# The gates of an mLSTM on a Trainium2 core: two batches of a step on two halves of the array's columns, and sizes and logarithms of the first half's gates a step sooner

## The reference, cut to what matters

```
ifg   = concatenate([q, k, v], axis=-1)           # 256 tokens x 768
ig    = (ifg @ igate_w.T + igate_b).T             # 8 heads x 256 tokens
fg    = (ifg @ fgate_w.T + fgate_b).T
log_f = log_sigmoid(fg)
cs    = cumsum(log_f, axis=1)
...                                                # maxima over cs and ig, exp, weighted sums
```

## Time and profile before

| | us |
|---|---|
| median of 3 runs | 1217.89 (1217.12 to 1219.18) |
| the profiled execution | 1213.67 |
| its span in the trace | 1212.1 |
| gates' stage, by the trace | 0 to 68.7 |
| busy in it: TensorE | 44.74 |
| VectorE | 47.01 |
| ScalarE | 18.86 |
| GpSimd | 11.81 |
| mean granted clock in it | 0.90 |
| the same after 68.7, up to 330 | 0.97 |

### The profile page before, as it was taken

One profiled execution on the slowest core, in us unless ns is written; L12 is line 12 of the kernel. 1 busy time (PEld: TensorE's weight loads), 2 busy tenths in 40 slices (PEclk: granted clock), 3 DMA queues, 4 the chain that ended last, 5 costly groups with the idle time before them and its releaser, 6 DMA issues. The chain is left out here.

```text
span 1212.1 us, 28045 instructions
## 1 busy us (share of the span) xinstructions
PE 1108.7 (91%) x9182; PEld 938.6 (77%) x9183; DVE 872.1 (72%) x1983; ACT 700.0 (58%) x1585; POOL 429.7 (35%) x567
## 2 busy tenths in 40 slices
PE   5869998999998899999999889789999999998987
PEld 1346665888887677777766478779999999997986
DVE  5758998766676788888887377457766666664665
ACT  1378996456572667666665543246655555553443
POOL 1237895531202011011130025664533333224654
PEclk8889999999998999999998988879999999998999
DMA  9246651000005446455453047657465555545664
GB/s 322 78 171 238 231 187 54 2 0 0 0 0 115 110 107 124 92 98 115 89 99 55 3 143 266 244 182 252 165 202 172 167 166 171 169 144 165 211 197 135
DMA packets 97678, 164.80 MB, mean 136 GB/s; under 512 B 12044, under 2 KB 72204, under 8 KB 95148
## 3 DMA queue, kind: packets, MB, share of 16 engines
q1 hardware_dynamic: 87756, 136.34, 38.3%
q0 software_dynamic: 9104, 26.49, 6.8%
q10 hardware_dynamic: 720, 0.71, 0.2%
HBM read 103.76 MB, written 33.69 MB: 113 GB/s over the span
## 5 line engine op out<-in xcount | busy, mean ns | idle before, releaser
L1822 DVE TENSOR_REDUCE c_mx<-d_bank 128x2 f32<-128x512 f32 x256 | 164.3, 685 | 18.4 <-PE d_bank L1974 18.0
L1737 ACT ACTIVATE c_probs<-c_t 128x512 f32<-128x512 f32 x248 | 134.7, 598 | 26.9 <-PE c_t L2000 26.1
L2923 ACT ACTIVATE d_g_full<-d_bank,d_e_bias 128x256 f32<-128x256 f32 x156 | 77.5, 497 | 98.6 <-PE d_bank L34 98.6
L32 PE MATMUL d_bank<-de_zt_hi,d_e_hi 128*128 128x256 f32 x312 | 91.1, 292 | 2.0 <-DVE de_zt_lo L2833 2.0
L34 PE MATMUL d_bank<-d_w_hi,d_g_lo 128*128 x312 | 88.2, 283 | 0.0
L33 PE MATMUL d_bank<-d_w_lo,d_g_hi 128*128 x312 | 88.2, 283 | 0.0
L32 PE MATMUL d_bank<-d_w_hi,d_g_hi 128*128 x312 | 88.1, 283 | 0.0
L33 PE MATMUL d_bank<-de_zt_lo,d_e_hi 128*128 128x256 f32 x312 | 87.8, 282 | 0.0
L34 PE MATMUL d_bank<-de_zt_hi,d_e_lo 128*128 128x256 f32 x312 | 87.3, 280 | 0.0
L1670 POOL CAST c_ct_hi<-c_c_raw 128x512 fp32r<-128x512 f32 x15 | 9.2, 611 | 210.0 <-PE c_misc L34 210.0
L3083 POOL DMA_INDIRECT d_w_lo<-d_y_rows,d_pos x64 | 64.3, 1005 | 53.1 <-ACT d_g_hi L3096 23.0
(11 more groups left out here) (424 smaller groups left out, 3763.4 us busy)
## 6 DMA issues: line engine op xcount, KB each, us to landing
d_e_raw<-in_w SPq DMA_DIRECT2D x39, 514.0 KB, 3.8
a_mb<-a_maxima SPq DMA_DIRECT2D x16, 1024.0 KB, 7.5
d_w_hi<-d_zt_kept SPq DMA_DIRECT2D x26, 512.0 KB
d_y_rows<-de_ys SPq DMA_DIRECT2D x39, 256.0 KB, 2.1
d_z_in<-d_z_rows POOLq DMA_DIRECT2D x37, 256.0 KB, 3.7
c_kt<-c_k_hi SPq DMA_DIRECT2D x64, 128.0 KB, 3.1
c_qt<-c_q_hi SPq DMA_DIRECT2D x64, 128.0 KB, 3.8
d_zt_kept<-d_w_hi SPq DMA_DIRECT2D x20, 256.0 KB
```

What stands on the lines that cost most here:

```text
L32: tensor.matmul(out, lhs_hi, rhs_hi, start=start, stop=False)
L1737: act.activation(probs[h % PR][:], t_bank(n, p, k), ACT.Exp).then_inc(exp_done, 1)
L1822: dve.tensor_reduce(mx[n % 2][:, :, k, p:p + 1], s_ps[h % SB], AX.X, ALU.max).then_inc(max_done, 1)
L2923: act.activation(g_full[:, m, :], hid[m][:, 0:TOK], ACT.Gelu, bias=bias[u][:, m:m + 1]).then_inc(gelu_full, 1)
```

## The change

`ROWS` is gone; `HALF` is 64. A step's two batches no longer lie side by side in the 512 columns of 40 partitions, but one on partitions 0 to 39 and the other on 64 to 103 of the same bank, 256 columns wide. Weights are padded to 64 columns. Every matmul of a part becomes two of 256 tokens, first batch and second batch in turn. ScalarE's gates are 128x256 instead of 40x512; `g_rows` and `last_rows` have 128 partitions and half the columns; the bias is loaded twice (two more small DMAs on ScalarE's queue, `gb_loaded` now 64). The placing DMAs are as many and as large, from other partitions. Apart from that, `sizes(0)` goes from i = 6 to i = 5, right behind `scale_by_tanh`, and `logarithms(0)` from behind `gates(5)` to ahead of it.

```diff
-    ROWS = LO + H
+    HALF = P // 2
...
-                queue.dma_start(dst[row:row + H, :], source[at:at + H, b * S:(b + 1) * S]).then_inc(placed, 16)
+                at_b = Mlstm.HALF * b + at
+                queue.dma_start(dst[row:row + H, :], source[at_b:at_b + H, :]).then_inc(placed, 16)
...
-        g_rows = sb("g_rows", [ROWS, (B - rows.LAST) * S])
+        g_rows = sb("g_rows", [P, (STEPS - 1) * S])
...
-            act.dma_start(gb[0:H, :], gate_cols[H:2 * H, :]).then_inc(gb_loaded, 16)
-            act.dma_start(gb[LO:ROWS, :], gate_cols[0:H, :]).then_inc(gb_loaded, 16)
+            for b in range(2):
+                for at, g in ((0, H), (LO, 0)):
+                    act.dma_start(gb[HALF * b + at:HALF * b + at + H, :], gate_cols[g:g + H, :]).then_inc(gb_loaded, 16)
...
-                act.activation(gate_rows(n), g_ps[n % 2][0:ROWS, :], ACT.Identity, bias=gb[:]).then_inc(rows_done, 1)
+                act.activation(gate_rows(n), g_ps[n % 2][:], ACT.Identity, bias=gb[:]).then_inc(rows_done, 1)
...
             for n in range(STEPS):
                 turn(n)
+                if n == 5:
+                    rows.logarithms(act, 0)
                 gates(n)
...
-                if n == 5:
-                    rows.logarithms(act, 0)
...
                 if i == 5:
                     scales(1)
                     scale_by_tanh()
-                if i == 6:
                     rows.sizes(dve, 0)
...
                 for c in range(2):
-                    pe.matmul(g_ps[n % 2][0:ROWS, :], wg[:, 2 + c, :], kt[n % KR][:, c, :], start=(c == 0), stop=False)
+                    for b in range(2):
+                        pe.matmul(g_ps[n % 2][HALF * b:HALF * (b + 1), :], wg[:, 2 + c, :], kt[n % KR][:, c, b * S:(b + 1) * S],
+                                  start=(c == 0), stop=False)
...
                 for c in range(2):
-                    mm = pe.matmul(g_ps[n % 2][0:ROWS, :], wg[:, c, :], qt_all[:, c, n * TOK:(n + 1) * TOK], start=False, stop=(c == 1))
+                    for b in range(2):
+                        mm = pe.matmul(g_ps[n % 2][HALF * b:HALF * (b + 1), :], wg[:, c, :], qt_all[:, c, (2 * n + b) * S:(2 * n + b + 1) * S],
+                                       start=False, stop=(c == 1))
```

More of the change, by code:

```diff
@@ L208, in __init__ @@
         self.cs, self.a, self.m, self.thr = sb("cs", [P, S]), sb("a", [P, S]), sb("m", [P, S]), sb("thr", [P, S])
-        self.last_rows = sb("last_rows", [Mlstm.ROWS, self.LAST * S])
+        self.last_rows = sb("last_rows", [P, S])
         self.placed = [sem(f"placed{k}") for k in range(3)]
@@ L304, in mlstm_gates @@
 def mlstm_gates(nc, src, x_all, tanh_g, ident, half_neg, ctx_t, gate_w, gate_b, qt_all, rows, lora, first):
-    B, S, D, H, J, LO, ROWS = Mlstm.B, Mlstm.S, Mlstm.D, Mlstm.H, Mlstm.J, Mlstm.LO, Mlstm.ROWS
+    B, S, D, H, J, LO, HALF = Mlstm.B, Mlstm.S, Mlstm.D, Mlstm.H, Mlstm.J, Mlstm.LO, Mlstm.HALF
     T = 2 * J
@@ L322, in mlstm_gates @@
         gate_raw = sb("gate_raw", [P, 4])
-        wg_raw, wg = sb("wg_raw", [P, 6, 2 * H]), sb("wg", [P, 4, ROWS])
-        gb = sb("gb", [ROWS, 1])
+        wg_raw, wg = sb("wg_raw", [P, 6, 2 * H]), sb("wg", [P, 4, HALF])
+        gb = sb("gb", [P, 1])
         kt = [sb(f"kt{u}", [P, 2, TOK]) for u in range(KR)]
@@ L335, in mlstm_gates @@
         tz = [[bank(f"tz{u}_{c}", [P, TOK]) for c in range(2)] for u in range(2)]
-        g_ps = [bank(f"g{u}", [P, TOK]) for u in range(2)]
+        g_ps = [bank(f"g{u}", [P, S]) for u in range(2)]
         tok_ps = bank("tok", [P, 2, J, rows.N])
@@ L355, in gate_rows @@
         def gate_rows(n):
-            return g_rows[:, n * TOK:(n + 1) * TOK] if n < PLACED else rows.last_rows[:]
+            return g_rows[:, n * S:(n + 1) * S] if n < PLACED else rows.last_rows[:]
         def place_rows(queue, n):
@@ L450, in _ @@
             act.wait_ge(up_loaded, 16)
-            act.wait_ge(gb_loaded, 32)
+            act.wait_ge(gb_loaded, 64)
             for n in range(STEPS):
                 turn(n)
+                if n == 5:
+                    rows.logarithms(act, 0)
                 gates(n)
```

## The result

| | median, us | runs |
|---|---|---|
| before | 1215.76 | 20 |
| changed | 1212.53 | 20 |

The changed kernel is 3.2 us faster by the medians. The ratio over all runs, which is not the ratio of the medians, is 0.9968, with a 95% interval of 0.9956 to 0.9979: that is 3.9 us, between 2.6 and 5.3. The forecast of 1214.1 has the right sign and the range holds the time, but it rests on a median of before of 1217.89, and twenty runs put that median at 1215.76. The profiled execution of the changed kernel took 1204.82, span 1203.2; it is the fastest of its twenty, by 3.3 us, so its rows show a good execution and not the middle one.

What follows compares the result with a forecast made beforehand. The gates' stage was bounded by the broadcast of the first maxima, later than VectorE's work. Cheaper parts, less the wait before sizes, plus earlier logarithms put the broadcast and first decay 3.8 us earlier: 1217.89 - 3.8 = 1214.1, range 1212.0 to 1217.9.

Steps and rivals of the forecast that it cites:

- The anchor: Whole-kernel time level: median before taken as 1217.89 us, 4.2 above the profiled time, from which the gain was subtracted.
- A part's price: TensorE's context or query part in the gates' stage: 0.96 us at full clock, 1.82 at half, saving 0.79 and 1.6.
- The first two gains: VectorE's two early waits for the turned maxima in the gates' stage: 1.65 us and another 2.57 earlier, 4.2 in all.
- The stall: VectorE's new wait for step 3's placing DMAs before the sizes: 2.3 us, up to 3.2 if half clock lasts.
- The idle time and the clock behind it: TensorE before turn 5: idle 4.7 us from 44.1 to 48.85, then half clock for 4 to 5 us.
- The later chain: SyncE's broadcast of the first maxima, leading to ScalarE's first decay: issued at 60.45 against 64.24, 3.8 us earlier.
- The logarithms ahead: ScalarE's logarithms before the gates of step 5: VectorE's scans start at 53.6 instead of 57.92, its 1.91 us wait gone.
- (a) and (b): VectorE's savings from cheaper parts in the gates' stage: 1.65 us at the first maxima, another 2.57 at the next.
- Carried 1 to 1: From the heads' start to the program's end: the first decay's gain of 3.8 us passes whole into the time.
- Half clock to the end: TensorE's clock stays low until the heads: gain 0 to 1 us; 23 in 100, with gains partly swallowed there.
- Full clock throughout: TensorE's clock never falls in the gates' stage: wait before sizes 1.1 us, total -6.2, 1211.7 us; 6 in 100.
- Rival 1: TensorE's column halves run one after the other, a part costing 1.75 us: +2.7, 1220.6 us; 9 in 100.

Runs made afterwards that it cites:

- four looks: The unaltered changed kernel, run and profiled in four sets of runs against the kernel before: ratios 0.9968, 0.9976, 0.999 and 0.9982.
- third look: The unaltered changed kernel run again as yardstick of a later batch, against the kernel before: 1209.31 us, ratio 0.999.
- fourth look: The unaltered changed kernel run once more as yardstick of another batch, against the kernel before: 1206.71 us, ratio 0.9982.
- second look: The unaltered changed kernel run again on one chip with the kernel before: 1173.70 us, ratio 0.9976.
- second look at the kernel before: The kernel before, unaltered, profiled once more: 1175.97 us, first decay at 70.90.
- two moves alone: Kernel before with sizes a step sooner and logarithms ahead of the gates of step 5, parts kept at 512 columns: 1181.63 us, ratio 1.0052.
- changed kernel with filler: Changed kernel plus unused TensorE matmuls, 20 ahead of turn 2 and 12 ahead of turn 5: 1206.41 us, ratio 0.997 against the kernel before.
- version with filler and the sizes at their old place: Changed kernel with sizes behind normalising 5 again, plus 20 unused matmuls ahead of turn 2: 1170.36 us, ratio 0.9945 against the kernel before.
- from two queues: Changed kernel with two of step 3's four placing DMAs issued by ScalarE instead of SyncE: one time of 1173.0 us.

## Why the prediction came out as it did

**The anchor: wrong, and the step that misses.** "The median shown is 4.2 above the profiled time; on that scale 1217.89 - 3.8 = 1214.1." The median of three was taken as the kernel's time. Their own spread was 2.1 us, and over twenty runs, between 1212.70 and 1220.20, the median is 1215.76. The term that was mis-sized is this level: 2.1 us too high. The same -3.8 from the right one gives 1212.0, 0.5 from the 1212.53 measured. Read as a time, the forecast is a gain of 1.7 us on the median of twenty, against 3.2 by the medians and 3.9 by the ratio. The likeliest band, 1212.8 to 1215.3, misses the time, and the range held it by only 0.5 at its lower end. As a difference, -3.8 fits this pair; in the three later batches the changed kernel gained 2.9, 0.9 and 2.5 us by the medians, so that it fits so well here is partly luck.

**A part's price: right.** 0.96 and 1.82 forecast, 0.91 and 1.76 measured; ScalarE's gates 0.44 and 0.47. Why was right too, that the halves work side by side: 1.78 on one half of the columns.

**The first two gains: right.** First scales 23.0, measured 22.66 in the trace after; second 41.6, measured 41.19.

**The stall: right in kind.** 2.3 forecast, "up to 3.2"; 1.81, 1.50, 2.41 and 2.78 in the four looks. The 4.59 from rows to `sizes`, carried over from before, was 4.67. What it was made of I had not asked; part of it was the load ahead.

**The idle time and the clock behind it: one of two ways.** "TensorE has then been idle from 44.1 ... to 48.85, 4.7 us. ... I take it as fallen." That is the third and the fourth look, 4.37 and 4.74. In the trace after and in the second look the clock had fallen a step sooner and was back for turn 5; in the trace after it fell once more for the two parts behind it. I had let it rise in step 3 and stay up through step 4, while behind the idle time of 1.88 and 2.39 us in front of turn 4, which the cheaper parts make, it fell in these two.

**The end of the stage: too late by 1.4 and 2.4 in two traces, too soon by 1.4 and 0.9 in two.** First decay 67.5 forecast; 66.14, 65.08, 68.88, 68.44, on average 67.1. The average is near since the two ways lie on either side of the forecast.

**The later chain: right.** Broadcast 60.45 forecast; 59.11, 58.13, 61.95 and 61.16. The decay follows it by 7.1 us before and by 6.8 to 7.5 in all the other traces.

**The logarithms ahead: right.** Scans 53.6 forecast without a wait; 52.58 to 54.97, no wait.

**The balance of the two moves: wrong by omission.** I wrote that the stall "gives back over half of (a) and (b)", and carried the moves as one with the halves. Sizes a step sooner only take: 0.3% more than without, in two batches. I never worked out the halves with the sizes left where they were.

**Carried 1 to 1: held within 2 us up to the LoRA stage, not shown to the end.** LoRA's first matmuls came 7.2 earlier in the trace after where the decays came 5.2 earlier; in the third look of the changed kernel 2.1 for 2.0, against the second look at the kernel before. The whole span came 8.9 earlier in the trace after, where 3.8 was forecast (1203.2, not 1208.3): 5.2 at the decay, 2.0 in the heads, and 1.7 behind them. Over the four looks the decay is 4.0 us earlier on average, the medians 0.9 to 3.2; whether all that the gates gain arrives at the end is open.

**The rivals.** The halves one after the other: excluded by the parts. Half clock to the end: not seen. Full clock throughout: its decay, -6.2, is 65.1, which the second look has (65.08) by another way. Rival 1's price for the stall at full part price was +2.7; the run of it cost 3.8 at the decay (71.32 to 75.07) and 5.1 in time. The clock was left out of it.

## What to carry to other kernels

Where a matmul has 64 output columns or fewer, two batches can run on the two column halves at almost half the price (here 0.91 and not 1.78 us a part, in either order), and it pays where another engine waits for the part. A consumer moved sooner is worth no more than its data's arrival: before moving the reader, look for a large transfer issued just ahead of the small one. And a forecast of a few microseconds is made as a difference: with three runs that spread by 2.1 us, their median is no anchor for a time to that accuracy.

## What the runs showed of the hardware

- Eight fp32 pieces of 128x64 by 256 columns cost 0.91 us on two halves and 1.78 on one at full clock; weight loads of the two halves overlap each other (0.5 us busy for 8 x 0.136, against 1.0 on one half).
- The clock's fall can sit at different places in executions of one program: after an idle time of 2.39 us turn 4 took 1.96 in one trace, after 1.88 it took 1.09 but the part behind it 1.96, after 1.55 both ran at full clock. The length of the idle time does not decide it: after 2.45 us turn 4 took 1.97 in the changed kernel with filler, and 1.09 in the version with filler and the sizes at their old place. What does decide it is not shown. With it the first decay moved between 65.08 and 68.88.
- With a load of 512 KB issued just ahead, the small transfers had landed 4.0 to 5.2 us after their rows were written (3.98 in the two moves alone, 5.16 from two queues); with the load behind them, in one trace, within 3.1.
